# A two-layer conditioned attention kernel: first keys in three passes, film rows by TensorE, an earlier value scale, and a reordered last unit

## The reference

```
xn = layernorm(x) * w + b
q  = softmax over each head's features (xn @ Wq + bq)        # 8 heads, then 16
k  = softmax over the tokens          (xn @ Wk + bk, masked)
v  = (xn @ Wv + bv), masked
y  = q @ (k^T v)                       per head, linear attention
scale, shift = split(silu(emb) @ W_emb + b_emb)   # "film", one row pair per batch
h  = silu(layernorm2(y) * (1 + scale) + shift)
x  = x + h @ W_out + b_out
```

## Time and profile before

| | |
|---|---|
| Median of 3 runs | 791.26 us (791.18 to 792.57) |
| Profiled execution | 791.3 us, its span 789.5 us |
| TensorE busy | 756.9 us, 96% of the span |
| VectorE busy | 688.4 us, 87% |
| ScalarE busy | 517.3 us, 66% |
| GpSimd busy | 444.9 us, 56% |

### The profile page before, as it was taken

How to read it: one execution, slowest core, us unless ns; L and a number is a source line. 1 busy time by engine, 2 the same in 40 slices (tenths; PEclk the granted TensorE clock), 3 DMA queues, 4 the chain that set the end, 5 groups by cost and what they waited for, 6 DMA issues and landing times.

```text
span 789.5 us, 18061 instructions
## 1 busy us (share of the span) xinstructions
PE 756.9 (96%) x6959; PEld 407.3 (52%) x6959; DVE 688.4 (87%) x1413; ACT 517.3 (66%) x1010; POOL 444.9 (56%) x437
## 2 busy tenths in 40 slices
PE   5996979999999999999999999999999999999997
PEld 3445446564464645546464554645455464646443
DVE  6897978789998999999988899988889988888976
ACT  5767585756657687686867676576657566571553
POOL 2356394654846758577664655636354544737253
PEclk9997999999999999999999999999999999999999
DMA  9958897765957659687594939779493959668282
GB/s 329 318 103 196 245 183 207 146 149 151 167 167 156 159 154 187 174 170 192 91 204 121 187 121 172 191 143 188 105 200 108 184 158 160 149 112 184 55 160 81
DMA packets 291510, 130.80 MB, mean 166 GB/s; under 512 B 261728, under 2 KB 262112, under 8 KB 291424
## 3 DMA queue, kind: packets, MB, share of 16 engines
q1 hardware_dynamic: 288688, 125.27, 71.1%
q10 hardware_dynamic: 2736, 4.39, 1.6%
HBM read 47.74 MB, written 16.88 MB: 82 GB/s over the span
## 4 chain that ended last, share of the span: by engine, by line
PE 50%; DVE 28%; ACT 8%; issue 7%; POOL 3%; DMA 3%; SPq 1%; DVEq 0%; ACTq 0%; POOLq 0%
PE ring L540 37%; DVE sb_k_or_qt L1058 5%; PE ring L589 3%; ACT sb_k_or_qt L1443 3%; DVE ring L1146 2%; DVE sb_y_stats L1150 2%; PE att_ps L686 2%; DVE sb_ht_parts L1163 2%; PE ring L595 2%; DVE sb_q_max L1091 2%; DVE ring L1093 2%; DMA sb_k_or_qt<-sb_tanh 2%; DVE ring L1088 2%; DVE sb_ht_parts L1175 2%; PE ring L733 1%
## 5 line engine op out<-in xcount | busy, mean ns | idle before, releaser
L540 PE MATMUL ring<-sb_w_hi,sb_xt_parts 128*128 128x512 f16 x1024 | 309.0, 379 | 0.0
L540 PE MATMUL ring<-sb_w_lo,sb_xt_parts 128*128 128x512 f16 x512 | 194.0, 379 | 0.0
L540 PEld LDWEIGHTS ring<-sb_w_hi,sb_xt_parts 128*128 128x128 f16 x1024 | 100.4, 98 | 123.4 <-issue 3.8
L540 PE MATMUL ring<-sb_w_hi,sb_ht_parts 128*128 128x512 f16 x512 | 155.9, 380 | 2.1 <-issue 1.7
L1709 POOL TENSOR_TENSOR sb_htok<-sb_ht_parts,sb_htok 128x512 f16<-128x512 f32 x60 | 75.3, 1276 | 131.1 <-ACT sb_htok L1480 131.1
L1725 POOL TENSOR_TENSOR sb_tanh<-sb_v_or_q,sb_kq_hi 128x512 f16<-128x512 f32 x64 | 74.2, 1159 | 86.2 <-ACT sb_kq_hi L1520 85.3
L540 PE MATMUL ring<-sb_w_lo,sb_ht_parts 128*128 128x512 f16 x256 | 97.1, 379 | 0.0
L1513 ACT ACTIVATE sb_v_or_q<-ring,sb_ln_one 128x512 f32<-128x512 f32 x64 | 43.9, 686 | 63.9 <-DVE ring L1093 63.9
L1700 POOL TENSOR_TENSOR sb_x<-sb_x,sb_bias_o 128x512 f32<-128x512 f32 x64 | 79.3, 1275 | 6.8 <-DVE sb_w_lo L979 6.8
L540 PEld LDWEIGHTS ring<-sb_w_hi,sb_ht_parts 128*128 128x128 f16 x512 | 50.1, 98 | 61.6 <-issue 2.6
L540 PEld LDWEIGHTS ring<-sb_w_lo,sb_xt_parts 128*128 128x128 f16 x512 | 50.1, 98 | 59.5 <-issue 0.7
(11 more groups left out here) (239 smaller groups left out, 1565.2 us busy)
## 6 DMA issues: line engine op xcount, KB each, us to landing
out<-sb_x SPq DMA_DIRECT2D x14, 1024.0 KB, 5.7
sb_rows_now<-film_rows SPq DMA_DIRECT2D x16, 512.0 KB, 4.6
sb_x<-out SPq DMA_DIRECT2D x8, 1024.0 KB, 5.4
sb_x<-in_x SPq DMA_DIRECT2D x7, 1024.0 KB, 5.5
sb_mask_add<-mask_terms SPq DMA_DIRECT2D x15, 256.0 KB, 6.1
sb_w_hi<-in_L_cond_W_emb SPq DMA_DIRECT2D x1, 1536.0 KB, 14.1
sb_w_lo<-in_L_cond_W_emb SPq DMA_DIRECT2D x1, 1536.0 KB, 14.9
sb_w_hi<-in_L_cond_film_emb_W ACTq DMA_DIRECT2D x1, 1536.0 KB, 7.6
```

The source lines that it names most:

```text
L540: last = nc.tensor.matmul(out, lhs, rhs, start=(n == 0), stop=(n == len(pairs) - 1))
```

## The change

On the left of each cut, the name of the list. The parts not shown are declarations and the lines that the new order replaces.

TensorE:

```diff
 # prelude, t == 3: the key peak sum goes between the transposes
+                elif t == 3:
+                    pe.wait_ge(consts_ready, 2)
+                    sum_w(0, K_)
 # first_keys: all four tiles, pass by pass
-                for i in range(2):
+                for i in range(C):          # pass 1: high-high
 ...
                 shift_parts(0, Q_)
                 pe.wait_ge(x0_lo_ready, T)
+                for i in range(C):          # pass 2: high-low
                     for c in range(C):
-                        nc.tensor.matmul(outs[i], hi[:, c, f], xt_lo[:, :, c, :], start=False, stop=False)
+                        nc.tensor.matmul(outs[i], hi[:, c, i * P:i * P + P], xt_lo[:, :, c, :], start=False, stop=False)
+                    if i == 1:
+                        sum_w(0, Q_)
+                for i in range(C):          # pass 3: low-high
 ...
+                    if i == 1:
+                        shift_sums(0, K_)
+                shift_sums(0, Q_)
+                shift_parts(0, V_)
+                sum_w(0, V_)
 # new: spread the first unit's film rows
+            def first_rows():
+                pe.wait_ge(film_ready, 1)
+                pe.wait_ge(q_exp, 4)
+                for c in range(C):
+                    at = c % 2 * 2 * P
+                    last = nc.tensor.matmul(ring[c // 2][:, at:at + 2 * P], ident[:, 32 * c:32 * c + 1].broadcast_to([P, P]),
+                                            film[:].rearrange("p n e -> p (n e)"), start=True, stop=True)
+                last.then_inc(first_rows_spread, 1)
 # first_unit
                     if i % 2 == 0:
                         film_product(0, i // 2)
+                    elif i == 1:
+                        shift_sums(0, V_)
-                project_tokens("V", 0, V_, xt_hi, xt_lo)
-                bound_film(0)
+                project_tokens("V", 0, V_, xt_hi, xt_lo, (0, 1, 2))
+                project_tokens("V", 0, V_, xt_hi, xt_lo, (3,), at=((4, lambda: bound_film(0)),))
+                first_rows()
                 first_attention()
                 attend(0)
+                sum_w(0, O_)                # was in step(1)
 # keys_by_halves(1) waits for first_rows_ready; the end:
-                output(u - 1, (3,), at=((2, lambda: turn_h(0)),))      # before product 8
+                output(u - 1, (3,), at=((4, lambda: turn_h(0)),))      # before product 4
-            turn_h(1)
-            last_output(0)
-            last_output(1, ((1, lambda: turn_h(2)),))                  # before product 5
-            last_output(2, ((2, lambda: turn_h(3)),))                  # before product 8
+            last_output(0, ((6, lambda: turn_h(1)),))
+            last_output(1, ((7, lambda: turn_h(2)),))
+            last_output(2, ((7, lambda: turn_h(3)),))
```

VectorE. The value bound of layer 0 becomes the largest entry of the raw bias, plus a bound on what the layernorm bias adds (from the weight peaks), plus the old bound of the product, so that both value scales come out of one `find_scale(0, V_)`; `v_scales` is left for layer 1 only:

```diff
 # find_peak(0, V_)
+                    link(nc.vector.tensor_tensor(bias_rows[:], rows, ln_bias_abs[:], ALU.mult))
+                    link(nc.vector.tensor_reduce(bias_row_sum[:], bias_rows[:], AX_X, ALU.add))
 # find_scale(0, V_)
+                    link(nc.vector.tensor_scalar(peak_all[:, 0, V_BOUND:V_BOUND + 1], sum_at(V_BOUND), v_bound[:, 0:1], TINY, ALU.add, ALU.max))
+                    power(0, V_, V_BOUND + 1, V_BOUND - V_)
 # fold(0, V_): the bias was scaled by ScalarE, the shift is scaled here
+                    dve.wait_ge(v_bias_up, 1)
+                    nc.vector.scalar_tensor_tensor(out=bias, in0=shift, scalar=scale_up[:, 0, V_BOUND:V_BOUND + 1], in1=bias, op0=ALU.mult, op1=ALU.add)
 # prelude
+            first_x_low(0)
             find_scale(0, K_)
-            for t in range(T):
+            for t in range(1, T):
                 first_x_low(t)
 # first_unit, new order
+                find_peak(0, Q_); find_scale(0, Q_); find_peak(0, V_)
+                masked_keys(0, 0); masked_keys(0, 1); fold(0, K_); masked_keys(0, 2); masked_keys(0, 3); key_shift(0)
+                fold(0, Q_); (v_bound from bias_v); find_scale(0, V_); (emb_half, emb_wide)
+                key_sums(0); queries(0, 0); split_low(V_); low_keys(0, 0..3); fold(0, V_)
+                queries(0, 1); queries(0, 2); queries(0, 3); values(0, 0)
+                rows_of_film(0); find_film_peak(0); values(0, 1); values(0, 2)
+                film_scales(0); query_sums(0, (0, 1)); values(0, 3); query_sums(0, (2, 3)); query_recip(0)
+                mask_attention(0); find_peak(0, O_)
+                attended_all(0, scales_of_output)   # find_scale(0, O_), output_scale(0) between its first moments and centre
 # step(1): find_scale(0, O_), output_scale(0) gone;  last_unit, behind the queries:
+                values(u, 2)
+                values(u, 3)
 # tail
+                for t in range(T):
+                    attended(LAST, t); y_statistics(LAST, t); y_moments(LAST, (t,)); centre(LAST, t)
+                    if t:
+                        last_h_low(t - 1)
+                    affine(LAST, t)
```

ScalarE, GpSimd and SP:

```diff
 # ScalarE, first_unit: scale_and_split(0, Q_) now ahead of x_squares(1); the exponents of the keys ahead of split_high(V_)
+                nc.scalar.activation(bias_v[:], bias_v[:], ACT.Copy, scale=scale_up[:, 0, V_BOUND:V_BOUND + 1]).then_inc(v_bias_up, 1)
+                high_values(0, (0,)); x_sums(2, (0,)); high_values(0, (1,)); x_sums(2, (1,))
+                high_values(0, (2,)); x_sums(2, (2, 3)); high_values(0, (3,))
+                copy_first_rows()                   # four copies of 256 columns from PSUM into rows_now
                 high_attention(0)
                 x_squares(2)
+                load_film_w(1, 0)                   # first half of the next film weight, was in step(1)
 # ScalarE, step(1)
+                    load_film_w(1, 1)
+                    scale_and_split(0, O_)          # now ahead of h_beside_keys(1)
 # ScalarE, high_values(LAST): full copy and cast for tiles 0 and 1 only, one activation for 2 and 3
-                    if u == LAST:
+                    if u == LAST and t < 2:
 # GpSimd, first_unit
-                pool.wait_ge(w_ready[0], 8)
-                add_bias(0)
 # GpSimd, step(1): both ahead of low_h(0)
+                    low_weight(0, O_, o0_ready)
+                    add_bias(0)
                 low_h(u - 1)
 # GpSimd, last_unit: low parts of value tiles 0 and 1 only
 # SP: load_rows(0) gone; store_table(0) moved from between two transposes of unit 0 to the start of step(1)
```

More of the change, by code:

```diff
@@ L428, in turn_k, with turn_x @@
                 turn(blocks_of(kt_lo), k_lo, k_lo_ready, 4 * (u + 1), kt_lo_ready)
-            def turn_x(u, j, parts=range(2)):
+            def turn_x(u, j):
                 sp.wait_ge(done["V" if u in Q_FIRST else "Q"], 4 * u + 2 * j + 2)
-                for n in parts:
-                    out, source, ready, turned = ((xt_hi, flat_x[0], xp_hi_ready, xt_hi_ready), (xt_lo, flat_x[1], xp_lo_ready, xt_lo_ready))[n]
+                for out, source, ready, turned in ((xt_hi, flat_x[0], xp_hi_ready, xt_hi_ready), (xt_lo, flat_x[1], xp_lo_ready, xt_lo_ready)):
                     turn(out[:, 2 * j:2 * j + 2].rearrange("p t c m -> p (t c) m"), source[:, 2 * j * D:2 * (j + 1) * D],
@@ L793, in step @@
                 project_keys(u, (2, 3))
-                def with_v(i):
-                    if u == 1 and i == 0:
-                        sum_w(0, O_)
                 if u == B:
                     pe.wait_ge(w_ready[1], 2)
-                project_tokens("V", u, V_, xt_hi, xt_lo, between=with_v)
+                project_tokens("V", u, V_, xt_hi, xt_lo)
                 if u == B:
@@ L885, in wait_here, with power @@
                 nc.vector.memset(spare[:, word:word + 1], 0.0)
[L887 to L889 removed]
+            def power(layer, n, end=None, step=1):
+                at = (slice(None), layer, slice(n, n + 1 if end is None else end, step))
                 link(nc.vector.tensor_scalar(scale_down[at].bitcast(I32), peak_all[at].bitcast(I32), EXP_BITS, None, ALU.bitwise_and))
@@ L1184, in attended_all @@
                     y_moments(u, pair)
+                    if pair[0] == 0:
+                        between()
                     for t in pair:
@@ L1546, in h_beside_keys, with copy_first_rows @@
                 high_h(u - 1, 3)
+            def copy_first_rows():
+                act.wait_ge(first_rows_spread, 1)
+                out = rows_now[:].rearrange("p n (j c e) -> p n j c e", j=2, c=C)
+                for c in range(C):
+                    at = c % 2 * 2 * P
+                    nc.scalar.copy(out[:, :, :, c, :], ring[c // 2][:, at:at + 2 * P].rearrange("p (n j e) -> p n j e", n=2, j=2)
+                                   ).then_inc(first_rows_ready, 1)
             def first_unit():
@@ L1785, in last_unit @@
                 low_h(u - 1)
-                for t in range(T):
-                    low_queries(u, (t,))
-                    low_values(u, (t,))
+                low_queries(u, (0,))
+                low_values(u, (0,))
+                low_queries(u, (1,))
+                low_values(u, (1,))
```

(1 more changed line is left out.)

186 lines of the change are left out of this document (82 added, 104 removed).

## The result

The changed kernel takes 787.4 us (median of 18 runs, 782.9 to 790.4), the kernel before, run beside it, 791.5 (789.6 to 792.7). The ratio is 0.9944 [0.9930, 0.9958]: 4.1 us gained, where 11.5 were forecast. 787.4 lies above the predicted range (777.8 to 784.6). The sign was right, the size wrong by nearly three. And the runs lie 7.5 us apart, those of before 3.0. Two executions of the experiments, one of e5 and one of the kernel before beside it, ran at mean clocks of 0.755 and 0.685 and took 986.3 and 1083.1 us; they are left out of every median, and the trace of e5, which is of the first of them, isn't read.

A forecast was written before the change was run, and what follows sets the result against it. TensorE was taken as the bound, busy 96% of the span with 32.6 us left. Gains of 3.5 (to unit 1's keys), 7.6 (unit 1) and 0.9 (last unit) make 12.0, less 0.7: 780.0 us, range 777.8 to 784.6.

The forecast's parts named there:

- the 0.7 held back for ties: Taken off the summed gain of 12.0 us for the ties named: centre, DMA issue, ports.
- a new wait of 0.6: Unit 0: TensorE's first query tile waits 0.6 us for VectorE's `fold(0, Q_)`, done at 32.5.
- the first piece: Start to the keys of unit 1: they start at 68.2, 3.5 us earlier.
- The clock: Rival, chance 0.22: clock falls again after thin work from 62.5 to 66.3, slowing `attend` and first keys; 782.8 us.
- By the rows nothing is added: Unit 1: GpSimd's bias addition beside a busy VectorE costs nothing extra from sharing ports, judged by profile rows.
- the second piece: Unit 1: its whole surplus beyond TensorE's 44.86 us of pure work goes, 7.6 us.
- the wait on GpSimd comes back: Rival, chance 0.17, unit 1: GpSimd's chain 3.3 late, 2 us of wait and 1.4 of clock loss; 783.4 us.
- GpSimd's chain: Unit 1: low weight, bias, low h and low values end at 98.2, wanted at 99.5, 1.3 us to spare.
- The last unit: Third piece: attention's 1.47 wait goes, first attended tile 0.8 earlier; gain 0.9 us, bounds -0.5 to 2.3.
- the 0.3 allowed for the last affine: Tail on VectorE: 0.3 allowed for the last affine's 1.02 us, of which 0.3 met GpSimd's additions.
- aren't touched: Units 2 to 14: not touched by the change, so left out of the sum of three pieces.
- the two rivals: The clock falls again (chance 0.22, 782.8 us) and the wait on GpSimd comes back in unit 1 (0.17, 783.4 us).

The follow-up runs named there:

- e5: Kernel e2 with unit 0's output bias added on GpSimd in unit 0, from the first query tile's bias on; 786.6 us, ratio 0.9940.
- e12: Changed kernel with 8 products that nothing reads in TensorE's wait ahead of the first query tile, the wait kept; 784.9 us, ratio 0.9918.
- e2: Changed kernel with the first query tile waiting only for the folded key bias, two film products one query tile later; 782.4 us, ratio 0.9881.
- e7: Kernel e2 with the last unit and the tail as they were before the change; 783.8 us, ratio 0.9911.
- e14: Kernel e9 with the tail's order and TensorE's transposes alone as before the change; 781.4 us, ratio 0.9876.
- e1: Changed kernel with GpSimd adding unit 0's output bias in unit 0, not in unit 1 ahead of low_h(0); 785.3 us, ratio 0.9919.
- e6: Kernel e2 with e5's bias place, the output weight's peak in halves, and unread products in two TensorE waits around the first attention; 785.8 us, ratio 0.9938.
- e9: Kernel e2 with unit 0's output bias added tile by tile in GpSimd's pauses beside VectorE's query tiles; 781.3 us, ratio 0.9876.

## Why the prediction was wrong

In the profiled execution the span is 784.7 against a forecast 778.2. The 6.5 are 3.1 in unit 0, 3.8 in unit 1 and 0.8 in the last unit, less 0.5 from units 2 to 14 and the 0.7 held back for ties. In unit 0 the queries start 0.7 late, their first tile takes 1.7 more at the low clock, and `attend(0)` and what follows to the keys take 4.0 instead of 3.1; 0.2 is made up between. In unit 1 the first keys at the low clock cost 1.3 (4.02 instead of 2.73), and TensorE waits 1.3, 0.5 and 0.4.

- **"a new wait of 0.6"**: 1.86. TensorE was ready at 31.3, not 31.9; `fold(0, Q_)` came 0.5 later, since two links of `find_peak(0, V_)` took 0.73 and 0.90 beside GpSimd's low query weight, not 0.2. I had named the wait and priced it as a wait only: this is the failed step of the first piece.
- **The clock**: the rival had it fall for the thin stretch from 62.5 to 66.3, and it fell at 67; I left out that a stand in front of the queries could do the same. That fall costs 1.5 up to the keys of unit 2 (e12), and the wait as much again (e2). In e7, with neither fall, keys of unit 1 start at 68.25, and the first piece had 68.2. That is in part luck: e7's queries start at 31.9, 0.6 before the forecast's 32.5.
- **"By the rows nothing is added"**: this is the failed step of the second piece. The addition in front of `low_h(0)` costs 2.5 in unit 1 (e7 and e14). The rows chosen for the price had VectorE working from PSUM beside them. Two other rows of the kernel before show the sharing, one beside `add_bias(0)`, one without:

```profile
38.00 1.20 DVE L1049 TENSOR_SCALAR sb_k_sum<-sb_k_sum 128x4 f32<-128x4 f32 x1 [0.18 <-ACT sb_k_or_qt L1443]
...
90.87 0.16 DVE L1049 TENSOR_SCALAR sb_k_sum<-sb_k_sum 128x4 f32<-128x4 f32 x1
```

  A duration has to be read with what its neighbour was doing. VectorE's lead of 4 us at the second key pair was gone at the low keys (93.10, before 92.03), about 1 of it in a wait for the fourth key tile, the rest beside the pair. ScalarE's gated h stands behind those keys, GpSimd's low h behind that, and its low values behind the low h, so attention(1) waited 1.31. The rival "the wait on GpSimd comes back" was right in place and sign, and its words allowed for VectorE; its price was for a full queue of ScalarE, and that was never full (its issues took 0.37 to 0.66). The Trainium skill, SBUF — State Buffer, SBUF: two separate sides, calls the pair of ports that VectorE and GpSimd share an exclusive lock, held for the whole instruction; it holds against VectorE instructions in a 2-port mode, or with two SBUF inputs where the GpSimd operation reads SBUF. The rows shown of e1, e6 and e9 agree, the 1.17 to 1.19 beside operations of 1.24 included; I had cited the rule from another page and set it aside.
- **GpSimd's chain** ("98.2"): its weight and bias ended at 92.1, forecast 88.6, half by the late start and half by the stretch. But it had 3.5 to spare there: `low_h(0)` starts with the gated h, not with GpSimd's own list.
- **The last unit**: the attention's wait went as forecast, and from the first attended tile to the last affine it took 13.77 (13.7 to 14.0 forecast). But the first attended tile came 0.6 earlier, not 0.8, behind TensorE's wait of 0.93 on the transposed low queries, and the 0.3 allowed for the last affine did not come (1.17 after 1.02). Even so TensorE's last twelve products start 58.5 behind the keys of unit 15, before 58.9. Most of that 0.4 went behind them: from their start to the end of the span it takes 6.4, before 6.1, though the work there is the same. VectorE, the tail:

```profile
760.26 0.70 DVE L1163 TENSOR_TENSOR ring<-ring,sb_q_recip 128x512 f32<-128x512 f32 x1 [1.02 <-PE ring L760]
...
774.03 1.17 DVE L1189 SCALAR_TENSOR_TENSOR sb_kt_or_y<-sb_kt_or_y,sb_y_rstd,sb_rows_now 128x512 f32<-128x512 f32 x1
```

- **Units 2 to 14 "aren't touched"**: their code isn't. Arriving earlier, unit 6 waits 0.6 to 2.9 us on a transfer for which it had waited 0.25. That and the number of clock falls are what the traces show of the spread; that they are all of it isn't shown.
- **The range** treated the two rivals as alternatives; both happened, and they add.

With the query wait gone and the addition beside work from PSUM, e9 takes 781.3, two of its four runs 780.5; the forecast for the change was 780.0. That it comes so near is no proof of the forecast's terms, since units 6 and 7 alone move by more. Shown by runs: the wait and its fall (3.0 up to unit 2, 5.0 in the median), the sharing (2.0 from the first query to unit 2, 2.5 in unit 1; e9's 1.1 in the median is within the intervals), the fall at 66 to 74 (1.7 up to unit 2 where VectorE isn't stretched). Not settled: why the landing of that transfer differs from one execution to another (nothing was tried on it), why the clock fell behind the stand at 33 in three traces and not in e1's, and the 2 us of e1's median.

## What to carry to other kernels

Price an operation that moves to GpSimd's free time by the VectorE operations it will lie beside: in these traces, operations from PSUM cost each other nothing, and of those from SBUF, the ones with two tensors and the small scale links on two or four columns could wait out a whole GpSimd operation, and it them. A new wait of TensorE in a thin stretch can cost, beyond itself, what the lower clock takes from the next products, so put the work whose operands are ready ahead of it, or fill it. And when a front becomes earlier, look for the first transfer further on that was in time by a little. Where single executions differ by as much as the edits, compare stretches of the traces, not only medians of a few runs.
